# Context attention: the last tile of 49 keys folded to 256 columns on two partition halves

## The chip, the cores and the metric

The kernel runs on one core of a Trainium2 chip. Its engines are TensorE (PE; its weight loads are listed as PEld), VectorE (DVE), ScalarE (ACT), GpSimd (POOL) and SyncE (SP, which here only issues DMAs). Each engine runs its own list of instructions in order and waits on semaphores. The metric is the device time of one execution in microseconds.

## What is computed

The whole program is two transformer layers. Each has a cross-attention to a context of 1601 vectors per batch, a self-attention and a feed-forward part. The change touches only the cross-attention ("context attention"), which is done twice. Cut to what matters:

```
B, H, HD = 16, 16, 32                        # batches, heads, width of a head
y_main = y[:, :-16, :]                       # 1585 of 1601 context vectors, 256 wide
k = _ln((y_main @ Wk + bk) per head, kn_w, kn_b)     # 512 wide: 16 heads of 32
v = (y_main @ Wv + bv) per head
s = einsum('bhqd,bhkd->bhqk', q, k) * SCALE
p = softmax(s)
ctx = einsum('bhqk,bhkd->bhqd', p, v)        # plus the attention to the 16 others, done elsewhere
out = ctx @ Wo + bo
```

## The kernel before

`context_attention` treats one batch after another. The 1585 keys of a batch are cut into KT = 13 tiles: twelve of P = 128 keys and a last one, the tail, of TAIL = 49. Everything is kept as sums of two float16 parts, high and low, so that float16 matmuls give nearly float32 results.

For each tile i there is a chain of steps, and the names are those of the lists below. TensorE makes the K and V products (`k`, `v`, function `project`): for each of 2 slices of the 256 inputs and 3 combinations of parts it multiplies 128 keys by 512 columns of the weights, as two matmuls of 64 keys on the two column halves of the array, into `ps_k` and `ps_v`, of which there is one each. VectorE scales and adds the bias (`kc`, L452), ScalarE squares (`sq`, L367), VectorE sums by head (`rd`, L460), ScalarE makes a first guess of the inverse root (`r`, L373 and L377), GpSimd improves it by a Newton step (`nw`, L300 to L310), ScalarE puts it into the last columns of `ps_h` (`rp`, L384), VectorE multiplies (`hat`, L467), ScalarE writes the high part (`kh`, L392), VectorE the low part (`kl`, L475), and a transposing DMA issued by SP (L263) turns both into `kk`, with the 512 columns of K on partitions, four groups of 128. V needs ScalarE's high (`vh`, L400) and VectorE's low part (`vl`, L482).

The attention goes in 14 units of two tiles by half of the heads (`s`, L652, then the exponentials `e` on ScalarE, L420 and L422, the low part of the exponential `lo` on GpSimd, L335, and the product with V `pv`, L679). Units 6 and 13 hold only the tail: heads 0 to 7 in unit 6, heads 8 to 15 in unit 13. Ahead of that, first scores (`m`, L618) and their maxima on VectorE (L493, L496) give a shift per query.

For the tail, function `rows(i)` gives 49 instead of 128, so each of its matmuls and of its steps on VectorE and ScalarE works on 49 partitions and all 512 columns. The matmuls of the tail's products use only one column half of the array.

The order on each engine is the table ORDER, written out by hand. The number after a name is the tile or unit, and each "-" behind it moves it to an earlier batch. K and V of the next batch are made while the attention of the present one runs. The first line of TensorE's list reads as below. The change leaves the table as it is.

```
PE: pv2-- v9-- k12-- s4-- m3-- v10-- pv3-- s5-- m4-- k0- v11-- pv4-- m5-- s6-- k1- v12-- s7-- pv5-- m6--
```

## Time and profile before

| | |
|---|---|
| timed runs | 3058.69, 3063.67, 3066.0 us (median 3063.67) |
| profiled execution | 3058.08 us |
| its span in the trace | 3056.3 us |
| PE, DVE, ACT, POOL busy | 91%, 84%, 74%, 53% |
| the two context attentions | 101 to 1076 us and 1758 to 2731 us of the span |
| one batch inside them | 57.0 us |

How to read the views. The windows view has a line for each stretch: its length, then for each engine its busy time with the number of its instructions in brackets, the granted share of TensorE's clock, the share of the DMA engines and GB/s. The timeline has start and duration in us, engine, line, operation, what it writes and reads, shapes (partitions x elements; for a matmul also rows*columns of the loaded weights) and the number of instructions that the row merges; in brackets the idle time of the engine before it, where it is long enough to be listed, and what ended it. The groups of instructions have line, engine, operation, names, shapes, count, then busy us and mean ns of one, then idle time before them. Neighbouring rows of VectorE and ScalarE overlap by about 0.08 to 0.1 us when the engine doesn't wait.

### The profile page before, as it was taken

What the parts mean: (1) busy time and instruction counts of PE and PEld (TensorE: products, weight loads), DVE (VectorE), ACT (ScalarE), POOL (GpSimd) and SP (SyncE); (2) the same over time, 40 slices, a digit from 0 to 9 for tenths busy, and PEclk for the clock granted to TensorE, in tenths of its full rate; (3) what the DMA queues carried; (4) which work ended last, traced back from release to release, by engine and by line L of the source; (5) the groups of instructions that cost most, each with busy time, mean ns of one, the idle gap of its engine ahead of it and who ended that gap; (6) DMA issues with size and microseconds to landing.
All of it is one profiled execution on the core that took longest, in us unless ns stands there. A gap on an engine that the chain in (4) does not pass through costs nothing. (4 is left out here: it accounts for less than half of the span.)

```text
span 3056.3 us, 103347 instructions
## 1 busy us (share of the span) xinstructions
PE 2793.6 (91%) x42025; PEld 1761.7 (58%) x42025; DVE 2558.9 (84%) x4146; ACT 2268.2 (74%) x4155; POOL 1612.8 (53%) x2006
## 2 busy tenths in 40 slices
PE   7789999999999778789996779999999999968889
PEld 3346666666666556577774435666666666645646
DVE  6599999999999656768885779999999999957752
ACT  5479999999999754446664448999999999963431
POOL 1257777777777543212223326777777777752200
PEclk9899999999999889899998989999999999979989
DMA  4354654554554244348885345545545555430020
GB/s 127 86 96 84 98 91 87 97 88 88 96 89 83 56 160 153 133 165 302 302 305 152 102 88 87 98 87 89 96 89 90 94 89 96 75 91 1 1 75 28
DMA packets 542754, 329.52 MB, mean 108 GB/s; under 512 B 459382, under 2 KB 504566, under 8 KB 536523
## 3 DMA queue, kind: packets, MB, share of 16 engines
q1 hardware_dynamic: 534314, 295.63, 43.7%
q0 software_dynamic: 7680, 25.17, 2.7%
q8 instruction: 337, 5.52, 0.7%
q10 hardware_dynamic: 288, 2.10, 0.2%
q14 instruction: 135, 1.10, 0.1%
HBM read 181.86 MB, written 36.09 MB: 71 GB/s over the span
## 5 line engine op out<-in xcount | busy, mean ns | idle before, releaser
L335 POOL TENSOR_TENSOR a_elo<-a_e 128x1024 f16<-128x1024 f32 x428 | 854.5, 1997 | 272.4 <-ACT a_e L422 272.4
L592 PE MATMUL a_ps_k<-l_wk,a_yh 128*64 128x512 f16 (+1 forms) x3200 | 580.2, 386 | 32.2 <-POOL a_yl L317 22.0
L592 PE MATMUL a_ps_v<-l_wv,a_yh 128*64 128x512 f16 (+1 forms) x3200 | 577.5, 384 | 17.4 <-DVE a_v L482 16.8
L493 DVE TENSOR_REDUCE a_mx<-a_ps_m 128x2 f32<-128x1024 f32 x384 | 466.7, 1215 | 13.3 <-PE a_ps_m L618 12.0
L420 ACT ACTIVATE a_e<-a_ps_t 128x1024 f32<-128x1024 f32 x428 | 409.7, 957 | 33.6 <-PE a_ps_t L652 27.3
L422 ACT ACTIVATE a_e<-a_ps_t 128x1024 f16<-128x1024 f32 x428 | 410.8, 960 | 0.0
L652 PE MATMUL a_ps_t<-a_qb,a_kk 64*128 64x128 f16 (+1 forms) x9672 | 351.1, 219 | 8.1 <-ACT a_e L422 7.8
L652 PEld LDWEIGHTS a_ps_t<-a_qb,a_kk 64*128 64x128 f16 (+1 forms) x9672 | 281.5, 96 | 120.1 <-issue 88.6
L592 PE MATMUL a_ps_k<-l_wk,a_yl 128*64 128x512 f16 (+1 forms) x1600 | 322.6, 383 | 0.0
L592 PE MATMUL a_ps_v<-l_wv,a_yl 128*64 128x512 f16 (+1 forms) x1600 | 320.6, 380 | 0.0
L592 PEld LDWEIGHTS a_ps_k<-l_wk,a_yh 128*64 128x64 f16 (+1 forms) x3200 | 191.3, 110 | 221.1 <-issue 49.4
L452 DVE SCALAR_TENSOR_TENSOR a_kc<-a_ps_k,l_bk 128x512 f32<-128x512 f32 (+1 forms) x416 | 282.7, 680 | 41.6 <-PE a_ps_k L592 40.8
L592 PEld LDWEIGHTS a_ps_v<-l_wv,a_yh 128*64 128x64 f16 (+1 forms) x3200 | 191.1, 110 | 204.6 <-DVE a_v L482 33.4
L400 ACT ACTIVATE a_v<-a_ps_v 128x512 f16<-128x512 f32 (+1 forms) x416 | 255.8, 615 | 59.7 <-PE a_ps_v L592 45.5
L392 ACT ACTIVATE a_khl<-a_ps_h,a_one 128x512 f16<-128x512 f32 (+1 forms) x416 | 284.0, 683 | 17.7 <-DVE a_ps_h L467 15.0
L482 DVE SCALAR_TENSOR_TENSOR a_v<-a_ps_v,a_v 128x512 f16<-128x512 f32 (+1 forms) x416 | 284.3, 683 | 12.2 <-ACT a_v L400 10.4
L467 DVE TENSOR_TENSOR a_ps_h<-a_kc,a_ps_h 128x512 f32<-128x512 f32 (+1 forms) x416 | 285.8, 687 | 5.0 <-ACT a_ps_h L384 2.5
L679 PE MATMUL a_ps_o<-a_v,a_e 128*64 128x65 f16 (+1 forms) x6480 | 268.9, 199 | 20.6 <-POOL a_elo L335 16.9
L475 DVE SCALAR_TENSOR_TENSOR a_khl<-a_ps_h,a_khl 128x512 f16<-128x512 f32 (+1 forms) x416 | 282.9, 680 | 2.7 <-ACT a_khl L392 2.4
L679 PEld LDWEIGHTS a_ps_o<-a_v,a_e 128*64 128x64 f16 (+1 forms) x6480 | 239.9, 113 | 77.1 <-issue 37.5
L367 ACT ACTIVATE a_sq<-a_kc 128x512 f32<-128x512 f32 (+1 forms) x416 | 260.7, 627 | 24.7 <-DVE a_kc L452 24.0
L460 DVE TENSOR_REDUCE a_var<-a_sq 128x16 f32<-128x512 f32 (+1 forms) x416 | 277.7, 674 | 0.0
(415 smaller groups left out, 5316.0 us busy)
## 6 DMA issues: line engine op xcount, KB each, us to landing
l_land<-in_ctx SPq DMA_DIRECT2D x96, 384.0 KB, 3.8
l_ob<-in_m_w SPq DMA_DIRECT2D x32, 1024.0 KB, 7.9
f_w<-in_m_w SPq DMA_DIRECT2D x32, 512.0 KB, 4.9
eo_dram<-f_e_eo SPq DMA_DIRECT2D x32, 512.0 KB, 4.6
l_land<-in_ctx SPq DMA_DIRECT2D x32, 433.0 KB, 4.4
a_kk<-a_khl SPq DMA_TRANSPOSE x416, 3.1
qs_dram<-p_q SPq DMA_DIRECT2D x32, 128.0 KB, 2.4
dca_dram<-p_od SPq DMA_DIRECT2D x16, 256.0 KB, 2.4
```

Of the source, the lines that this page charges most:

```text
L335: pool.tensor_tensor(rest[0:r, :, 0:w], full[0:r, :, 0:w], high[0:r, :, 0:w], ALU.subtract)\
L392: act.activation(khl[0:r, n % 2, 0, :], ps_h[0:r, :], ACT.Identity, bias=one[0:r, 0:1])\
L420: act.activation(full[0:r, :, 0:w], src[0:r, :, 0:w], ACT.Exp)
L422: act.activation(high[0:r, :, 0:w], src[0:r, :, 0:w], ACT.Exp).then_inc(e_done, 1)
L452: dve.scalar_tensor_tensor(out=kc[0:r, kc_slot(at, i), :], in0=ps_k[0:r, :], scalar=1.0 / WSCALE, in1=bk[0:r, :], op0=ALU.mult, op1=ALU.ad ...
L467: dve.tensor_tensor(ps_h[0:r, :].rearrange("p (h d) -> p h d", d=HD), kc[0:r, kc_slot(at, i), :].rearrange("p (h d) -> p h d", d=HD), ps_h ...
L475: dve.scalar_tensor_tensor(out=khl[0:r, n % 2, 1, :], in0=ps_h[0:r, :], scalar=1.0, in1=khl[0:r, n % 2, 0, :], op0=ALU.add, op1=ALU.subtract)\
L482: dve.scalar_tensor_tensor(out=v[0:r, at.nbp, i, :, VLO:OW], in0=ps_v[0:r, :].rearrange("p (h d) -> p h d", d=HD), scalar=1.0 / WSCALE, in ...
L493: dve.tensor_reduce(mx[:, g, :, c], ps_m[:, :, :], AX.X, ALU.max).then_inc(mx_done, 1)
L592: m = pe.matmul(out[half:half + h, :], part[:, n % 2, c, o + half:o + half + h], w[:, wpart, c, :], start=(c == 0 and a == 0), stop=(c == ...
L652: t = pe.matmul(dst[0:rows(i), r, col:col + P], kk[d, at.bp, kpart + g, k], qb[d, at.bp, g, qpart, :, :].rearrange("p a q -> p (a q)"), st ...
L679: t = pe.matmul(ps_o[q, a * OW:a * OW + w], part[k, r, col + 64 * par:col + 64 * par + 64], v[k, at.bp, i, 2 * pair + par, 0:w], start=fir ...
```

## The change

Half of the tail's columns move to other partitions. Keys 0 to 48 with heads 0 to 7 (columns 0 to 255) stand on partitions 0 to 48, and the same keys with heads 8 to 15 (columns 256 to 511) on partitions 64 to 112. So `rows` gives 113 for the tail, and a new function `width` gives 256 columns for it instead of 512. `project` makes each step of the tail with two matmuls, 49 keys by 256 columns of the weights, one on each column half of the array. The steps `kc`, `sq`, `rd`, `hat`, `kh`, `kl`, `vh` and `vl` of the tail work on 256 columns. The bias in this form is a new tile `bt`, made by two copies on ScalarE at the start. The high and low parts of K stand side by side in 512 columns, so that one transposing DMA of 128 rows by 512 columns (before: 64 by 1024) brings them into a new tile `kt`. Scores, exponentials and values of unit 6 read and write partitions 0 to 48, those of unit 13 partitions 64 to 112, with the same numbers and sizes of matmuls. On GpSimd the low part of unit 13 runs over partitions 0 to 112. The instructions of each engine keep their order.

```diff
+        kk = sb("kk", [P, 2, 2 * GROUPS, (KT - 1) * P], F16)
+        kt = sb("kt", [P, 2, GROUPS, P], F16)
+        bt = sb("bt", [P, D // 2])
...
-            return P if i < KT - 1 else TAIL
+            return P if i < KT - 1 else 64 + TAIL
+
+        def width(i):
+            return D if i < KT - 1 else D // 2
+
+        def heads(i):
+            return width(i) // HD
+
+        def tail_rows(half):
+            return slice(64 * half, 64 * half + TAIL)
...
-            return (P, 512) if len(tiles_of(j)) == 2 else (TAIL, 256)
+            return (slice(0, P), 512) if len(tiles_of(j)) == 2 else (tail_rows(j // TPAIRS), 256)
...
                     if b >= 2:
                         sp.wait_ge(s_done, (b - 2) * UNITS + TPAIRS + i // 2 + 1)
-                    sp.dma_start_transpose(kk[:, b % 2, :, i * P:i * P + r],
-                                           khl[0:r, n % 2].rearrange("p a d -> p (a d)")).then_inc(turned[n % 2], 16)
+                    if i < KT - 1:
+                        sp.dma_start_transpose(kk[:, b % 2, :, i * P:(i + 1) * P],
+                                               khl[:, n % 2].rearrange("p a d -> p (a d)")).then_inc(turned[n % 2], 16)
+                    else:
+                        sp.dma_start_transpose(kt[:, b % 2], khl[:, n % 2, 0, :]).then_inc(turned[n % 2], 16)
...
+                for half in range(2):
+                    q = slice(64 * half, 64 * half + 64)
+                    act.activation(bt[q, :], bk[q, half * D // 2:(half + 1) * D // 2], ACT.Copy).then_inc(bt_ok, 1)
...
-                    dve.scalar_tensor_tensor(out=kc[0:r, kc_slot(at, i), :], in0=ps_k[0:r, :], scalar=1.0 / WSCALE,
-                                             in1=bk[0:r, :], op0=ALU.mult, op1=ALU.add).then_inc(kc_done, 1)
+                    bias, w = (bk, D) if i < KT - 1 else (bt, D // 2)
+                    if n == KT - 1:
+                        dve.wait_ge(bt_ok, 2)
+                    dve.scalar_tensor_tensor(out=kc[0:r, kc_slot(at, i), 0:w], in0=ps_k[0:r, 0:w], scalar=1.0 / WSCALE,
+                                             in1=bias[0:r, :], op0=ALU.mult, op1=ALU.add).then_inc(kc_done, 1)
...
                     dve.wait_ge(rp_done, n + 1)
-                    dve.tensor_tensor(ps_h[0:r, :].rearrange("p (h d) -> p h d", d=HD),
-                                      kc[0:r, kc_slot(at, i), :].rearrange("p (h d) -> p h d", d=HD),
-                                      ps_h[0:r, RSTD:D].unsqueeze(2).broadcast_to([r, H, HD]), ALU.mult)\
+                    w, hh = width(i), heads(i)
+                    dve.tensor_tensor(ps_h[0:r, 0:w].rearrange("p (h d) -> p h d", d=HD),
+                                      kc[0:r, kc_slot(at, i), 0:w].rearrange("p (h d) -> p h d", d=HD),
+                                      ps_h[0:r, w - hh:w].unsqueeze(2).broadcast_to([r, hh, HD]), ALU.mult)\
                        .then_inc(hat_done, 1)
...
-                            for half in range(0, r, 64):
-                                h = min(64, r - half)
-                                m = pe.matmul(out[half:half + h, :], part[:, n % 2, c, o + half:o + half + h], w[:, wpart, c, :],
-                                              start=(c == 0 and a == 0), stop=(c == KC - 1 and a == 2))
+                            for half in range(2):
+                                if i < KT - 1:
+                                    to, at_y, cols = slice(64 * half, 64 * half + 64), o + 64 * half, slice(0, D)
+                                else:
+                                    to, at_y, cols = tail_rows(half), o, slice(half * D // 2, (half + 1) * D // 2)
+                                m = pe.matmul(out[to, 0:width(i)], part[:, n % 2, c, at_y:at_y + to.stop - to.start],
+                                              w[:, wpart, c, cols], start=(c == 0 and a == 0), stop=(c == KC - 1 and a == 2))
...
                                 for r in range(2):
                                     d = slice(64 * r, 64 * r + 64)
-                                    t = pe.matmul(dst[0:rows(i), r, col:col + P], kk[d, at.bp, kpart + g, k],
+                                    keys = kk[d, at.bp, GROUPS * kpart + g, i * P:(i + 1) * P] if i < KT - 1 \
+                                        else kt[d, at.bp, 2 * kpart + gl, to]
+                                    t = pe.matmul(dst[to, r, col:col + P], keys,
                                                   qb[d, at.bp, g, qpart, :, :].rearrange("p a q -> p (a q)"),
```

## Rows read from the trace of the kernel before

**Rows 1.** The page, part 1: busy time of TensorE and of VectorE over the span.

```profile
PE 2793.6 (91%) x42025; PEld 1761.7 (58%) x42025; DVE 2558.9 (84%) x4146; ACT 2268.2 (74%) x4155; POOL 1612.8 (53%) x2006
```

**Rows 2.** Windows: PE, PEld, DVE, ACT, POOL busy; one batch, and the first attention's fill.

```profile
357.31:414.31 57.00, 56.92 (x1096) 34.89 (x1094) 56.30 (x91) 54.07 (x101) 43.10 (x55) 1.00 0.53 92
...
130.00:186.50 56.50, 42.57 (x346) 18.12 (x344) 54.61 (x81) 32.71 (x73) 16.98 (x41) 1.00 0.49 94
```

**Rows 3.** Timeline of PE and PEld: end of a V product, the tail's K product, next scores.

```profile
380.36 0.10 PEld L592 LDWEIGHTS a_ps_k<-l_wk,a_yh 128*49 128x49 f16 x1
...
380.36 0.39 PE L592 MATMUL a_ps_v<-l_wv,a_yh 128*64 128x512 f16 x2
380.57 0.38 PE L592 MATMUL a_ps_k<-l_wk,a_yh 128*49 128x512 f16 x1
...
381.65 0.38 PE L592 MATMUL a_ps_k<-l_wk,a_yh 128*49 128x512 f16 x1
381.96 0.23 PE L652 MATMUL a_ps_t<-a_qb,a_kk 64*128 64x128 f16 x2
```

**Rows 4.** Timeline of PE: 256 columns in the feed-forward part; a values unit, first and last.

```profile
1407.10 5.08 PE L2903 MATMUL f_e_ps_g<-f_e_gt,f_e_a 128*128 128x256 f16 x45
...
362.91 0.20 PE L679 MATMUL a_ps_o<-a_v,a_e 128*64 128x65 f16 x2
...
363.38 0.19 PE L679 MATMUL a_ps_o<-a_v,a_elo 128*64 128x33 f16 x2
```

**Rows 5.** Groups by shape on VectorE: longest and shortest tail form, a reduction of 256.

```profile
L467 DVE TENSOR_TENSOR a_ps_h<-a_kc,a_ps_h 49x512 f32<-49x512 f32 x32 | 21.7, 677 | 0.0
...
L460 DVE TENSOR_REDUCE a_var<-a_sq 49x16 f32<-49x512 f32 x32 | 21.4, 668 | 0.0
...
L1036 DVE TENSOR_REDUCE p_dmx<-p_ps_ds 128x16 f32<-128x256 f32 x16 | 6.7, 421 | 13.8 <-PE p_ps_ds L1363 13.8
```

**Rows 6.** Groups by shape on ScalarE: two tail forms, a copy of 256 columns.

```profile
L392 ACT ACTIVATE a_khl<-a_ps_h,a_one 49x512 f16<-49x512 f32 x32 | 21.6, 674 | 2.0 <-DVE a_ps_h L467 2.0
...
L400 ACT ACTIVATE a_v<-a_ps_v 49x512 f16<-49x512 f32 x32 | 19.3, 604 | 11.3 <-PE a_ps_v L592 11.2
...
L1222 ACT ACTIVATE p_pdt<-p_ps_pt 128x256 f32<-128x256 f32 x16 | 6.1, 380 | 4.3 <-PE p_ps_pt L1316 4.3
```

**Rows 7.** Timelines of ACT, PE and POOL, from the tail's V product to the values.

```profile
392.00 0.21 ACT L377 ACTIVATE a_r<-a_lnv 49x16 f32<-49x16 f32 x1
392.23 0.38 PE L592 MATMUL a_ps_v<-l_wv,a_yh 128*49 128x512 f16 x1
...
392.65 0.60 ACT L400 ACTIVATE a_v<-a_ps_v 49x512 f16<-49x512 f32 x1 [0.43 <-PE a_ps_v L592]
...
396.03 0.39 PE L618 MATMUL a_ps_m<-a_kk,a_qm 64*128 64x512 f16 x2
396.42 0.84 PE L652 MATMUL a_ps_t<-a_qb,a_kk 64*128 64x128 f16 x24
...
399.32 2.14 POOL L335 TENSOR_TENSOR a_elo<-a_e 128x1024 f16<-128x1024 f32 x1 [0.74 <-ACT a_e L422]
...
401.14 0.39 PE L618 MATMUL a_ps_m<-a_kk,a_qm 64*128 64x512 f16 x2
401.61 0.22 PE L679 MATMUL a_ps_o<-a_v,a_e 128*64 128x65 f16 x2
```

**Rows 8.** Timelines of ACT, DVE and PE, from an exponential to a V product.

```profile
371.53 1.03 ACT L420 ACTIVATE a_e<-a_ps_t 128x1024 f32<-128x1024 f32 x1
...
381.89 0.69 DVE L482 SCALAR_TENSOR_TENSOR a_v<-a_ps_v,a_v 128x512 f16<-128x512 f32 x1
...
382.95 0.41 PE L592 MATMUL a_ps_v<-l_wv,a_yh 128*64 128x512 f16 x2
```

**Rows 9.** The tile `kk`: time from issue to landing of its transposing DMAs.

```profile
DMA to landing us min/median/max: 2.6/3.1/5.7
```

More of the change, by code:

```diff
@@ L297, in newton_step @@
                     n, u, nt, r = at.nb * TPAIRS + p, (at.nbp * TPAIRS + p) % 2, len(tiles_of(p)), rows(2 * p)
[L298 removed]
+                    hh = heads(2 * p)
+                    v2, r2, a2, b2 = (t[0:r, u, 0:nt, 0:hh] for t in (var, r0, na, nb_))
                     pool.wait_ge(r0_done, n + 1)
[L300 removed]
+                    pool.tensor_tensor(a2, v2, eps[0:r, 0:nt * hh].rearrange("p (t h) -> p t h", h=hh), ALU.add)\
                         .then_inc(newton[0], 1)
@@ L334, in p_low @@
                     wait_values(pool, at, j)
-                    pool.tensor_tensor(rest[0:r, :, 0:w], full[0:r, :, 0:w], high[0:r, :, 0:w], ALU.subtract)\
+                    pool.tensor_tensor(rest[0:r.stop, :, 0:w], full[0:r.stop, :, 0:w], high[0:r.stop, :, 0:w],
+                                       ALU.subtract)\
                         .then_inc(lo_done, 1)
@@ L366, in square @@
                     need(act, red_done, n - 1)
-                    act.activation(sq[0:r, t, :], kc[0:r, kc_slot(at, i), :], ACT.Square, scale=SCALE).then_inc(sq_done, 1)
+                    w = width(i)
+                    act.activation(sq[0:r, t, 0:w], kc[0:r, kc_slot(at, i), 0:w], ACT.Square, scale=SCALE).then_inc(sq_done, 1)
                 def guess(at, p):
@@ L372, in guess @@
                     act.wait_ge(red_done, at.nb * KT + 2 * p + nt)
-                    act.activation(lnv[0:r, u, 0:nt, :], var[0:r, u, 0:nt, :], ACT.Ln, bias=eps[0:r, 0:1])\
+                    hh = heads(2 * p)
+                    act.activation(lnv[0:r, u, 0:nt, 0:hh], var[0:r, u, 0:nt, 0:hh], ACT.Ln, bias=eps[0:r, 0:1])\
                         .then_inc(ln_done, 1)
@@ L391, in k_high @@
                         act.wait_ge(turned[n % 2], 16 * (n // 2))
-                    act.activation(khl[0:r, n % 2, 0, :], ps_h[0:r, :], ACT.Identity, bias=one[0:r, 0:1])\
+                    w = width(i)
+                    act.activation(khl[0:r, n % 2, 0, 0:w], ps_h[0:r, 0:w], ACT.Identity, bias=one[0:r, 0:1])\
                         .then_inc(kh_done, 1)
@@ L459, in variance @@
                     need(dve, newton[4], at.nb * TPAIRS + p - 1)
-                    dve.tensor_reduce(var[0:r, (at.nbp * TPAIRS + p) % 2, i % 2, :], sq[0:r, t, :].rearrange("p (h d) -> p h d", d=HD), AX.X, ALU.add)\
+                    dve.tensor_reduce(var[0:r, (at.nbp * TPAIRS + p) % 2, i % 2, 0:heads(i)],
+                                      sq[0:r, t, 0:width(i)].rearrange("p (h d) -> p h d", d=HD), AX.X, ALU.add)\
                        .then_inc(red_done, 1)
@@ L474, in k_low @@
                     dve.wait_ge(kh_done, n + 1)
-                    dve.scalar_tensor_tensor(out=khl[0:r, n % 2, 1, :], in0=ps_h[0:r, :], scalar=1.0,
-                                             in1=khl[0:r, n % 2, 0, :], op0=ALU.add, op1=ALU.subtract)\
+                    w = width(i)
+                    part = khl[0:r, n % 2].rearrange("p a d -> p (a d)")[:, w:2 * w]
+                    dve.scalar_tensor_tensor(out=part, in0=ps_h[0:r, 0:w], scalar=1.0,
+                                             in1=khl[0:r, n % 2, 0, 0:w], op0=ALU.add, op1=ALU.subtract)\
                        .then_inc(kl_done, 1)
@@ L540, in low @@
                     wait_values(dve, at, j)
-                    dve.tensor_tensor(rest[0:r, :, 0:w], full[0:r, :, 0:w], high[0:r, :, 0:w], ALU.subtract)\
+                    dve.tensor_tensor(rest[r, :, 0:w], full[r, :, 0:w], high[r, :, 0:w], ALU.subtract)\
                        .then_inc(low_done, 1)
@@ L644, in scores @@
                     for i in tiles_of(j):
-                        k = slice(i * P, i * P + rows(i))
+                        to = slice(0, P) if i < KT - 1 else tail_rows(half)
                         for gl in range(2):
@@ L667, in values @@
                     for i in tiles_of(j):
-                        k = slice(0, rows(i))
+                        k = slice(0, P) if i < KT - 1 else tail_rows(half)
+                        h0 = 0 if i < KT - 1 else H // 2 * half
                         for gl in range(2):
```

36 lines of the change are left out of this document (18 added, 18 removed).

## The prediction

> **What bounds the kernel now.** I read the page's busy shares first, then the windows view over one batch, then the timeline of single engines inside that batch, and last the groups of instructions by shape. The page gives TensorE 91% and VectorE 84% of the span [rows 1]; these are means over very different stages, so they say only where to look. The windows view says more. In the two context attentions one batch follows another every 57.00 us, and in such a stretch TensorE is busy for 56.92, VectorE for 56.30, ScalarE for 54.07 and GpSimd for 43.10 us, at a granted clock of 1.00 [rows 2]. Two engines are full, and a third nearly so. A busy TensorE proves little by itself, since the ends of matmuls are modelled; the spacing of their starts is the proof. A pair of 64-row matmuls of 512 columns holds the engine for 0.21 us (380.36 to 380.57), and so does each of the six single matmuls of the tail's product, which start from 380.57 to 381.65; the next group, which uses another split of the array, starts 0.31 us after the last [rows 3]. I followed such starts through the batch, and nearly all are that dense. The exceptions are two: the scores of 396.42 come 0.39 us after a pair of 512 columns that needs 0.22, and the values of 401.61 come 0.47 us after one that needs 0.31 (rows 3's step with a change of split) [rows 7]. That is 0.17 + 0.15 = 0.32 us of waiting. TensorE's own work is thus 57.00 - 0.32 = 56.68 us a batch.
>
> **What the change takes away on TensorE.** Before, the tail's K and V products are six matmuls each of 49 rows by 512 columns: 6 x 0.216 = 1.30 us each, half the array's columns idle. Now they are six pairs of 49 rows by 256 columns, on the two halves of the array. What does a pair of 256 columns cost? No row shows exactly that. The nearest rows: a matmul of 256 columns of the same type on the whole array, 45 in 5.08 us, so (5.08 - 0.27) / 44 = 109 ns from start to start; and the pairs of the values, 64 rows each with 65 and 33 columns, 16 pairs from 362.91 to 363.38, so 31 ns a pair with two weight loads and different moving data on the two halves [rows 4]. Two halves with different data do run beside each other, loads and all, and 31 ns is far below 109. From above, the two matmuls of a pair one after the other would be 218 ns, which is what is there now; from below, 107 ns, half of 0.214. I take 109, nearest to both rows. A product then takes 6 x 0.109 = 0.65 us, and a batch saves 2 x 0.65 = 1.29 us. Scores, first scores and values of the tail keep their numbers and sizes of matmuls, only partitions and array halves differ: nothing.
>
> Weighed against a page: the rows of the values show 15 ns per matmul with a weight load each [rows 4]. The Trainium skill, "TensorE: Matmul & The Clock Gate", section "Back-to-back issue gap", says that in a real stream of load and matmul the spacing is about 81 ns per matmul at 128 columns and 131 at 512. A straight line between them gives an estimate of 98 ns at 256, hence 12 x 98 = 1.18 us for a product and only 0.24 us saved a batch on TensorE. It speaks against this change; I give it little weight because 15 ns is far under its floor.
>
> **On VectorE.** Five instructions a batch shrink from 512 to 256 columns (centred K, variance, normalised K, low part of K, low part of V). The tail forms last 668 to 677 ns; a reduction of 256 columns lasts 421 ns [rows 5]. 5 x (0.672 - 0.424), with 0.003 added for operands in PSUM, is 1.24 us. VectorE is bound in the fill, where it is busy for 54.61 of 56.50 us [rows 2]; the saving counts there in place of TensorE's.
>
> **On ScalarE.** Square, high part of K and high part of V shrink. The forms last 674 (K) and 604 ns (V); a copy of 256 columns out of PSUM lasts 380 [rows 6]. That is 0.22 us for V; for the other two, by the same slope, 0.21 each: 0.65 us a batch. The exponentials keep 512 columns.
>
> **Small things.** The 8 instead of 16 heads in the guess, the root and GpSimd's Newton steps save tens of nanoseconds beside other work: 0. GpSimd's low part for the second tail unit reads 113 partitions instead of 49 at the same width; its time goes by width, and it is idle for 14 us of the batch [rows 2]: 0. The bias is copied twice at the start of each attention (two ScalarE copies of 256 columns, 0.8 us at [rows 6]), while the first context chunk is still on its way, and VectorE waits for it only at its first tail, long after: 0; if that cover were gone it would be 2 x 0.8 = 1.6 us in all. The tail's transposing DMA moves 128 rows of 512 columns instead of 64 rows of 1024, the same bytes and half of a usual one; landings of all sizes take 2.6 to 5.7 us, 3.1 in the middle [rows 9]. I take 0; the bound is 0.4 us either way, the space between 2.6 and the usual 3.1, and it isn't waited for at once. No instruction changes its place in any engine's order.
>
> **Which loops are left.** All engines run fixed lists, so the period is that of the slowest loop through the semaphores. Four are close.
> (a) TensorE alone: 56.68 - 1.29 = 55.39 us.
> (b) The loop with the waits seen today: V tail product (last start 392.23) -> V's high part on ScalarE at 392.65, which waited 0.43 us for it -> ScalarE's list up to the scores' exponentials -> scores 396.42 -> exponentials -> GpSimd 399.32 for 2.14 us, ending 401.46 -> values 401.61 -> TensorE to the next batch [rows 7]. Its length is the full 57.00. It loses both products' 1.29 and V's 0.22: 55.49.
> (c) The same without TensorE's tail: ScalarE's own list is busy until 392.21, 0.02 us before that last product starts, and V's high part can move up by the 0.53 us from there to 392.65 plus the usual overlap of 0.1 [rows 7]. So 57.00 - 0.53 - 0.22 (V) - 0.21 (square) = 56.04, less what ScalarE idles elsewhere on the way, which its timeline lets me estimate at up to 0.24: 55.80 to 56.04.
> (d) ScalarE runs without a break from its exponential at 371.53 to the root that VectorE's normalised K waits for, VectorE's low part of V follows at 381.89 and ends at 382.58, and the next V product starts at 382.95, where TensorE would take it from about 382.64 on [rows 8]. That loop has 0.31 us to spare, misses the K tail product and loses only the V one: 57.00 - 0.31 - 0.65 = 56.04; on its way it also skips the 0.32 us of waits or takes V's 0.22: 55.72 to 55.82.
> VectorE alone is below: 56.30 - 1.24 = 55.06, or 55.76 if all its idle 0.70 us stays [rows 2].
> So the period falls to between 55.4 and 56.04, and the late ones decide: I take 55.85, a gain of 1.15 us. Late next is ScalarE, not TensorE.
>
> **The sum.** Each attention does 16 tails, two attentions 32: 32 x 1.15 = 36.8 us. The profiled execution took 3058.1 us (span 3056.3), hence 3021.3. The timed runs lie at 3058.7, 3063.7 and 3066.0, the median 5.6 above the profiled one. I add half of that difference: 3024 us.
>
> **The rivals.**
> 1. A wait that I didn't find takes the saving's place. ScalarE and VectorE are idle for 2.9 and 0.7 us of a batch, in small pieces [rows 2], and fixed lists may interlock otherwise with other durations. Half of the gain remains: 32 x 0.5 = 16 us, 3045 on the same footing. For it: (c) and (d) are already such loops. Against: in every loop that I followed some tail instruction stands. Chance 0.11, spread over gains from 8 to 22 us.
> 2. The pair of 256 columns takes 218 ns, one after the other; the change doesn't do on TensorE what it says. (a) stays at 56.68, the gain is 0.32 x 32 = 10 us: 3051. By the page above, with its 0.24 us, it would be 0.56 x 32 = 18 us and 3043. Against both: rows 4. Chance 0.05.
> 3. Slower: the weight loads come into the open. A load of 49 columns lasts 0.10 us [rows 3] and is hidden today under 0.216 us of streaming; now two of them have to hide under 0.109. If each matmul waited for its own, a pair would take 2 x (0.109 + 0.10) = 0.42 us, 12 pairs 2.4 us more a batch, so 56.68 + 2.4 = 59.1, and 32 x 2.1 = 67 us: 3128. It turns into a loss once a pair takes over 0.216 + 0.32 / 12 = 0.243 us. Against: the values' pairs, 31 ns with their loads. Chance 0.03.
> 4. Nothing moves, because what holds the period is a loop with no tail instruction at all: within 6 us of 3061. Against: all four loops above have one. Chance 0.03.
>
> **How the numbers follow.** The forecast (gains of 22 to 51 us, periods of 55.4 to 56.3) has 0.78. Gains of under 0.2% (6 us, about what a measurement of this kernel can tell from no change) come from rival 4 and the end of rivals 1 and 2. Faster 0.93, same 0.04, slower 0.03. The range reaches from 3058.7 - 51 = 3008 to 3066 - 22 = 3044, and takes in part of rival 1.
>
> **What would show it.** In the profile after: starts of the tail's products 0.11 us apart by pairs; VectorE's tail forms near 425 ns and ScalarE's near 385 to 460; windows of about 55.85 us, with TensorE waiting some 0.4 us more per batch than today, in front of the V product of (d) or the scores and values of (b); V's high part of the tail no longer idle for 0.43 us. Wrong would be: pairs at 0.2 us (rivals 2, 3), or windows over 56.3 us with pairs at 0.11 (rival 1).

## The result, and the profile after

The changed kernel takes 3028.76 us (median of 4 runs, 3025.69 to 3031.59) against 3062.49 us for the kernel before: a ratio of 0.989, with a 95% interval of 0.9873 to 0.9907. Its profiled execution took 3027.51 us, with a span of 3025.7. A second comparison (run `after_again`, 5 runs against 23 of the kernel before), gave 3030.5 against 3056.84 us, a ratio of 0.9923 (0.991 to 0.9936): 26 us saved and not 34. The first ratio flatters the change somewhat. The prediction said 3024, between 3008 and 3044. The time and the direction hold, and the small saving that it announced on each engine is there; the step from these savings to the period of a batch does not hold, and most of what follows is about that step.

First the sizes. The page's busy line, which answers [rows 1]:

```profile
PE 2762.7 (91%) x42409; PEld 1765.6 (58%) x42409; DVE 2521.2 (83%) x4146; ACT 2247.9 (74%) x4159; POOL 1613.7 (53%) x2006
```

The windows view over one batch of each context attention, which answers [rows 2] (PE, PEld, DVE, ACT, POOL busy, each with its count, the granted clock, the DMA share, GB/s):

```profile
351.31:407.36 56.05, 55.74 (x1108) 34.85 (x1104) 55.08 (x90) 53.30 (x101) 42.98 (x55) 1.00 0.56 93
687.95:744.01 56.06, 55.68 (x1108) 34.81 (x1106) 55.14 (x91) 53.41 (x101) 43.06 (x55) 1.00 0.52 93
```

VectorE's 1.24 us a batch is gone from 56.30 (55.08 and 55.14 now), ScalarE's 0.65 from 54.07 (53.30 and 53.41). The timeline of TensorE at the tail's K product, which answers [rows 3]:

```profile
711.21 0.28 PE L626 MATMUL a_ps_k<-l_wk,a_yh 128*49 128x256 f16 x2
711.32 0.28 PE L626 MATMUL a_ps_k<-l_wk,a_yl 128*49 128x256 f16 x2
711.43 0.39 PE L626 MATMUL a_ps_k<-l_wk,a_yh 128*49 128x256 f16 x4
...
711.97 0.84 PE L689 MATMUL a_ps_t<-a_qb,a_kk 64*128 64x128 f16 x24
```

The two matmuls of a pair start together, and pair follows pair by 0.11 us (711.21, 711.32, 711.43). The scores start 0.76 us after the first pair, where the tail of before needed 381.96 - 380.57 = 1.39. The difference is 0.63 to 0.65 us for a product, as predicted. The groups by shape on VectorE, ScalarE and GpSimd (busy us, mean ns of one, idle before), which answer [rows 5] and [rows 6]:

```profile
L495 DVE TENSOR_TENSOR a_ps_h<-a_kc,a_ps_h 113x256 f32<-113x256 f32 x32 | 13.3, 416 | 0.4 <-ACT a_ps_h L406 0.4
...
L486 DVE TENSOR_REDUCE a_var<-a_sq 113x8 f32<-113x256 f32 x32 | 13.0, 406 | 0.0
...
L415 ACT ACTIVATE a_khl<-a_ps_h,a_one 113x256 f16<-113x256 f32 x32 | 15.3, 477 | 1.0 <-DVE a_ps_h L495 1.0
...
L387 ACT ACTIVATE a_sq<-a_kc 113x256 f32<-113x256 f32 x32 | 14.6, 457 | 0.0
...
L423 ACT ACTIVATE a_v<-a_ps_v 113x256 f16<-113x256 f32 x32 | 12.5, 391 | 2.4
...
L350 POOL TENSOR_TENSOR a_elo<-a_e 113x512 f16<-113x512 f32 x30 | 34.8, 1161 | 0.9 <-ACT a_e L445 0.9
L350 POOL TENSOR_TENSOR a_elo<-a_e 49x512 f16<-49x512 f32 x30 | 34.5, 1150 | 17.1 <-ACT a_e L445 17.1
```

The lines shown for VectorE are its longest and its shortest tail form; all five lie between 406 and 416 ns (424 was taken). 113 partitions instead of 49 cost GpSimd 11 ns. The idle time of 11.3 us ahead of the tail's high part of V [rows 6] is down to 2.4, as loop (b) said it would be.

Now the period. It is read from the start of the reduction of the maxima (L534), which comes once a batch, here on VectorE's timeline:

```profile
687.95 0.17 DVE L534 TENSOR_REDUCE a_mxx<-a_mx 128x8 f32<-128x32 f32 x1
...
744.01 0.17 DVE L534 TENSOR_REDUCE a_mxx<-a_mx 128x8 f32<-128x32 f32 x1
```

So this batch takes 56.06 us. Over 26 batches (13 of each attention) the most frequent value is 56.04 to 56.07, the mean 56.15; before, 57.00 and 57.03. A batch of the most frequent length is called calm below. The gain is 0.95 us in a calm batch and 0.88 in the mean, where 1.15 was predicted. Of the span's 30.6 us, 2 x 15 periods make 26.6. The other 4 us lie outside these periods, and the profiles show how little they mean. From the last values of the first attention to the first K product of the second, a stretch in which only the two bias copies are new, TensorE's timeline has 689.4 us before and 689.1 in the changed kernel, but 691.5 in a second profile of the same changed kernel (span 3027.0), and 684.5 to 693.3 over all 14 profiles. The first attention's fill, from its first K product to its first L534, has 78.8 us before and 78.3 and 77.0 in the two profiles of the changed kernel. So single times can differ by several us for reasons that no change here touches, and the experiments are read by their periods.

Two waits stand on TensorE's timeline where there was slack (time to spare) before:

```profile
712.65 0.38 PE L653 MATMUL a_ps_m<-a_kk,a_qm 64*128 64x512 f16 x2
713.25 0.41 PE L626 MATMUL a_ps_v<-l_wv,a_yh 128*64 128x512 f16 x2 [0.22 <-DVE a_v L513]
...
714.36 0.38 PE L626 MATMUL a_ps_v<-l_wv,a_yh 128*64 128x512 f16 x2
714.75 0.22 PE L717 MATMUL a_ps_o<-a_v,a_e 128*64 128x65 f16 x2
```

The V product of tile 10 starts 0.60 us after the first scores instead of 0.31, that is loop (d) of the prediction, announced. The values of unit 3 start 0.39 us after the last group of that product; before they started 0.21 after it. That wait, 0.18 us, was in no step of the prediction. It leads back through GpSimd and ScalarE, whose timelines are:

```profile
709.48 0.26 POOL L315 TENSOR_TENSOR a_na<-a_var,a_eps 128x32 f32<-128x32 f32 x1 [0.24 <-ACT a_r L398]
...
710.71 0.25 POOL L325 TENSOR_TENSOR a_rstd<-a_r,a_na 128x32 f32<-128x32 f32 x1
710.92 1.59 POOL L332 TENSOR_TENSOR a_yl<-l_land,a_yh 128x768 f16<-128x768 f32 x1
712.47 2.14 POOL L350 TENSOR_TENSOR a_elo<-a_e 128x1024 f16<-128x1024 f32 x1
```

```profile
702.16 1.02 ACT L443 ACTIVATE a_e<-a_ps_t 128x1024 f32<-128x1024 f32 x1
...
709.17 0.23 ACT L398 ACTIVATE a_r<-a_lnv 128x32 f32<-128x32 f32 x1
709.30 0.67 ACT L415 ACTIVATE a_khl<-a_ps_h,a_one 128x512 f16<-128x512 f32 x1
```

ScalarE's root guess ends at 709.40, GpSimd refines it, then makes the low part of the context (ends 712.51), then the low part of the exponentials of unit 3 (712.47 + 2.14 = 714.61), and the values start 0.14 us later. GpSimd is idle for 13 us of the batch, and still it is on the path here: between those two points its list holds nothing but the refining steps, each waiting for the one before it, and the two low parts. Before, the same steps left a little to spare, as the timelines of GpSimd and TensorE of before show:

```profile
381.84 2.14 POOL L335 TENSOR_TENSOR a_elo<-a_e 128x1024 f16<-128x1024 f32 x1
```

```profile
384.06 0.38 PE L592 MATMUL a_ps_v<-l_wv,a_yh 128*64 128x512 f16 x2
384.27 0.20 PE L679 MATMUL a_ps_o<-a_v,a_e 128*64 128x65 f16 x2
```

**The loop through GpSimd** closes like this (a loop is a chain of steps and hand-overs from one batch to the same step of the next; the period can't be shorter than the longest): scores of unit 8 -> their exponentials on ScalarE (727.00 to 728.94) -> their low part on GpSimd (729.02 to 731.16) -> values of unit 8 (731.30) -> TensorE to the scores of unit 1 of the next batch -> ScalarE without a break from the exponentials of unit 1 to the root -> GpSimd as above -> values of unit 3 -> TensorE with the tail's V product to the scores of unit 8. Its length can be had from the trace of before: 57.00 us less the 0.15 us that the values of unit 3 had to spare (384.27 against 381.84 + 2.14 + 0.14) and the 0.17 us that the scores waited at 396.42 [rows 7] makes 56.68. It bypasses the K product and VectorE altogether, so all it loses is one product: 56.68 - 0.65 = 56.03 us, and 56.04 is the period measured.

It isn't alone. **A loop through the exponentials of unit 4** has the same stretch of ScalarE and no step of GpSimd for unit 3: ScalarE goes on from the root to the exponentials of unit 4, and their end lets TensorE start the scores of unit 5; from there on it is the loop above. ScalarE's and TensorE's timelines of before:

```profile
382.16 0.71 ACT L392 ACTIVATE a_khl<-a_ps_h,a_one 128x512 f16<-128x512 f32 x1
382.85 1.03 ACT L420 ACTIVATE a_e<-a_ps_t 128x1024 f32<-128x1024 f32 x1
383.77 1.01 ACT L422 ACTIVATE a_e<-a_ps_t 128x1024 f16<-128x1024 f32 x1
```

```profile
384.87 0.84 PE L652 MATMUL a_ps_t<-a_qb,a_kk 64*128 64x128 f16 x24
```

and of the changed kernel:

```profile
714.26 1.06 ACT L445 ACTIVATE a_e<-a_ps_t 128x1024 f16<-128x1024 f32 x1
```

```profile
715.37 0.40 PE L689 MATMUL a_ps_t<-a_qb,a_kk 64*128 64x128 f16 x8
```

In the changed kernel these scores start 0.05 to 0.06 us after the exponentials end (714.26 + 1.06), with nothing to spare. Before, they had 0.03 (384.87 against 383.77 + 1.01 + 0.06), and the exponentials had waited some 0.12 themselves: they start 0.69 us after the high part of K, where 0.57 is usual (713.35 - 712.78 in the changed kernel). So this loop was 57.00 - 0.03 - 0.12 - 0.17 = 56.68 long, and with one product less it is again 56.03. Both loops could be read from the trace of before, and in the changed kernel both bind at once.

### The profile page after: what moved, and what is told of

Same layout as the page of the kernel before. It is cut to its first block and busy times, and to the rows that moved or that the text cites. A ratio compares the mean times of both kernels' runs of the same rounds, so it can differ in the third digit from the quotient of the medians.

```text
span 3025.7 us, 104119 instructions
## 1 busy us (share of the span) xinstructions
PE 2762.7 (91%) x42409; PEld 1765.6 (58%) x42409; DVE 2521.2 (83%) x4146; ACT 2247.9 (74%) x4159; POOL 1613.7 (53%) x2006
## 5 line engine op out<-in xcount | busy, mean ns | idle before, releaser
L626 PE MATMUL a_ps_k<-l_wk,a_yh 128*64 128x512 f16 (+1 forms) x3328 | 564.1, 378 | 32.2 <-POOL a_yl L332 21.9
L626 PE MATMUL a_ps_v<-l_wv,a_yh 128*64 128x512 f16 (+1 forms) x3328 | 561.4, 376 | 22.1 <-DVE a_v L513 20.9
L689 PE MATMUL a_ps_t<-a_qb,a_kk 64*128 64x128 f16 x8928 | 319.3, 219 | 8.1 <-ACT a_e L445 8.0
L689 PEld LDWEIGHTS a_ps_t<-a_qb,a_kk 64*128 64x128 f16 x8928 | 260.9, 95 | 84.1 <-issue 53.8
L478 DVE SCALAR_TENSOR_TENSOR a_kc<-a_ps_k,l_bk 128x512 f32<-128x512 f32 x384 | 261.0, 680 | 43.8 <-PE a_ps_k L626 43.0
L415 ACT ACTIVATE a_khl<-a_ps_h,a_one 128x512 f16<-128x512 f32 (+1 forms) x416 | 276.8, 665 | 16.0 <-DVE a_ps_h L495 14.3
L513 DVE SCALAR_TENSOR_TENSOR a_v<-a_ps_v,a_v 128x512 f16<-128x512 f32 (+1 forms) x416 | 275.5, 662 | 14.1 <-ACT a_v L423 11.8
L495 DVE TENSOR_TENSOR a_ps_h<-a_kc,a_ps_h 128x512 f32<-128x512 f32 (+1 forms) x416 | 276.9, 666 | 9.0 <-ACT a_ps_h L406 6.9
L505 DVE SCALAR_TENSOR_TENSOR a_khl<-a_ps_h,a_khl 128x512 f16<-128x512 f32 (+1 forms) x416 | 275.2, 662 | 4.2 <-ACT a_khl L415 2.1
L486 DVE TENSOR_REDUCE a_var<-a_sq 128x16 f32<-128x512 f32 (+1 forms) x416 | 269.6, 654 | 0.0
```

Source lines behind the costliest of these rows:

```text
L415: act.activation(khl[0:r, n % 2, 0, 0:w], ps_h[0:r, 0:w], ACT.Identity, bias=one[0:r, 0:1])\
L486: dve.tensor_reduce(var[0:r, (at.nbp * TPAIRS + p) % 2, i % 2, 0:heads(i)], sq[0:r, t, 0:width(i)].rearrange("p (h d) -> p h d", d=HD), AX ...
L495: dve.tensor_tensor(ps_h[0:r, 0:w].rearrange("p (h d) -> p h d", d=HD), kc[0:r, kc_slot(at, i), 0:w].rearrange("p (h d) -> p h d", d=HD), ...
L505: dve.scalar_tensor_tensor(out=part, in0=ps_h[0:r, 0:w], scalar=1.0, in1=khl[0:r, n % 2, 0, 0:w], op0=ALU.add, op1=ALU.subtract)\
L513: dve.scalar_tensor_tensor(out=v[0:r, at.nbp, i, 0:hh, VLO:OW], in0=ps_v[0:r, 0:w].rearrange("p (h d) -> p h d", d=HD), scalar=1.0 / WSCAL ...
L626: m = pe.matmul(out[to, 0:width(i)], part[:, n % 2, c, at_y:at_y + to.stop - to.start], w[:, wpart, c, cols], start=(c == 0 and a == 0), s ...
```

## The experiments

Each ratio is to the kernel before on the same chip; its median was 3055.9 to 3056.8 us there, lower than the 3062.49 of the first comparison. `rd_full`, `k3_full`, `wide_v`, `wide_k` and `swap_pool` ran once each, so their times say little. Periods are from starts of L534, have 26 batches each behind them and hold for calm ones. The expectations call a wait of TensorE a stay.

**The parts one by one.** `pe_wide` undoes TensorE's part: the first half's matmuls have 512 columns again (the second half's still run beside them), and the unused columns are computed for nothing.

```
-    m = pe.matmul(out[to, 0:width(i)], part[:, n % 2, c, at_y:at_y + to.stop - to.start],
+    wide = half == 0
+    wc = D if wide else width(i)
+    if wide:
+        cols = slice(0, D)
+    m = pe.matmul(out[to, 0:wc], part[:, n % 2, c, at_y:at_y + to.stop - to.start],
```

> Of the changed kernel, TensorE's part undone alone: in the tail's K and V products the matmul on the lower half of the array runs over all 512 columns of the weights again (the upper 256 columns of its result are never used), so a pair holds TensorE for 0.216 us instead of 0.109; VectorE and ScalarE keep their 256 columns. The changed kernel has a period of 56.05 us per batch and 3028.8 us in all. Theory E (a loop through VectorE's tail variance and the low part of K, tile 11, sets the period; it misses both tail products on TensorE): the period rises only until TensorE's own work, 55.39 + 1.29 = 56.68 us, is the longest: 56.7 us, +20 us, about 3049. Rival D (the loop over VectorE's low part of V, tile 9, and the V product of tile 10): it has the tail's V product in it, 56.04 + 0.65 = 56.7, the same. Rival V (TensorE doesn't matter any more): 56.05 and 3029.

Measured: 3049.34 us, ratio 0.9973 (0.9961 to 0.9985). The period, again from VectorE's timeline (582.24 to 639.06), is 56.82 us, 0.12 over what two of the theories expected: VectorE's and ScalarE's 1.9 us together are worth 0.18 us a batch. What is left is TensorE with its one wait, for GpSimd's low part ahead of the values of unit 8: 57.00 - 0.17 = 56.83.

`va_full` keeps TensorE's part and undoes the others: the tail's five steps on VectorE and three on ScalarE run over 512 columns of 113 partitions, half of them without meaning (the same edit in most steps; the bias and the high part of K are read twice over).

```
-    w = width(i)
+    w = D
...
-    w, hh = width(i), heads(i)
+    w, hh = D, H
```

> The other way round: TensorE's part of the change alone. The tail's products are folded as in the changed kernel, but all of VectorE's and ScalarE's tail steps (centred K, variance, normalised K, high and low parts of K and V, square) run over 512 columns again, the upper 256 unused. Theory E: +0.26 us for the tail's variance and +0.19 for the centred K, which stand in the loop: 56.3 to 56.5 us per batch, +8 to +14 us on 3028.8. Rival D: none of the two stands in it, but V's high part (+0.21) may, by the loop over ScalarE: 56.05 to 56.25, 0 to +6 us. Rival A (TensorE alone counts): 56.05, 3029.

Measured: 3051.56 us, ratio 0.9989 (0.9979 to 0.9998), period 56.69. The expectation missed, its highest theory (E) by 0.2 to 0.4 us; the timelines of TensorE and VectorE show why:

```profile
673.57 0.39 PE L664 MATMUL a_ps_m<-a_kk,a_qm 64*128 64x512 f16 x2
674.17 0.41 PE L637 MATMUL a_ps_k<-l_wk,a_yh 128*64 128x512 f16 x2 [0.21 <-DVE a_kc L479]
```

```profile
672.84 0.69 DVE L501 TENSOR_TENSOR a_ps_h<-a_kc,a_ps_h 128x512 f32<-128x512 f32 x1
673.43 0.68 DVE L479 SCALAR_TENSOR_TENSOR a_kc<-a_ps_k,l_bk 128x512 f32<-128x512 f32 x1
```

Here a K product waits for the centred K of the tile before (ends 674.11), 0.3 us beyond the usual 0.31 after the scores, and that wait is not there in the changed kernel. VectorE at its old length seems to have a loop of its own at 56.69; no run shows that loop by itself. By its period this kernel should be some 4 us faster than `pe_wide`, and it took 2 us more: that is within what the work outside the batches varies by. So TensorE alone gains 0.31 us a batch, the other two alone 0.18, and both together 0.95: in nearly every loop of before, the other engine's saving was needed too.

**Which TensorE work counts.** `wide_v` and `wide_k` widen one of the two products only.

```
+    wide = half == 0 and done is v_done        # wide_v
+    wide = half == 0 and done is k_done        # wide_k
```

> The changed kernel with only the tail's V product on TensorE wide again (a pair holds it for 0.216 us, 0.65 us more a batch). After the first runs there are two candidates for the 56.04 us: theory F, a loop that goes through GpSimd's low part of exponential unit 3, the values of unit 3 on TensorE, the tail's V product, the scores of unit 8 and back through ScalarE and GpSimd; and theory E, the loop through VectorE's tail variance (by the runs with VectorE's steps undone, 55.99 us long). F has the tail's V product in it: 56.04 + 0.65 = 56.7 us. E doesn't: TensorE's own list with its stay at GpSimd, 55.55 + 0.65 = 56.2 us, would be the longest.

> The same with only the tail's K product wide, which stands ahead of the values of unit 3, where loop F enters TensorE. Theory F: the period rises only to TensorE's own 56.2 us, +0.15. A theory in which TensorE's work as such sets the period: 56.05 + 0.65 = 56.7 us, the same as with the V product.

Both add 32 x 0.65 us of TensorE time; the groups by shape of `wide_v` and of `wide_k` show one kind of product at 512 columns each:

```profile
L630 PE MATMUL a_ps_v<-l_wv,a_yh 128*49 128x512 f16 x128 | 43.3, 379 | 1.2 <-DVE a_v L513 1.2
```

```profile
L630 PE MATMUL a_ps_k<-l_wk,a_yh 128*49 128x512 f16 x128 | 43.3, 379 | 0.3 <-DVE a_kc L478 0.3
```

Measured: 3041.39 us and a period of 56.69 with the wide V product, 3035.16 us and 56.19 with the wide K product. The V product comes back in full (+0.65), the K product with 0.15. That is what the loop through GpSimd asks for, which holds the V product and bypasses the K product: 56.04 + 0.65 = 56.69, and 56.19 is TensorE with its one wait, 56.83 - 0.65 = 56.18. A TensorE that is slow as such would have given the same for both, and the loop through VectorE 56.2 for the V product. The loop through the exponentials of unit 4 also holds the V product and bypasses the K product, so these two runs can't tell it from the one through GpSimd.

**A step of VectorE.** `rd_full` sums the tail's variance over 512 columns, `k3_full` does its centred, normalised and low K so.

```
-    sq[0:r, t, 0:width(i)].rearrange("p (h d) -> p h d", d=HD), AX.X, ALU.add)
+    sq[0:r, t, :].rearrange("p (h d) -> p h d", d=HD), AX.X, ALU.add)
```

> The changed kernel with one instruction a batch undone: the tail's variance on VectorE reduces 512 columns again (16 heads, the upper 8 unused), 0.26 us more. It runs between the low part of K of tile 8 and that of tile 11. Theory E: the period rises by all of it, 56.05 to 56.31 us. Rival D: nothing, 56.05, since the low part of V of tile 9 comes ahead of it and the rest of that loop runs on TensorE. Rival A: 56.05.

> The changed kernel with three of VectorE's tail steps undone: centred K, normalised K and the low part of K run over 512 columns again, 0.8 us more in all. Normalised K and the low part of the tail come after the low part of K, tile 11, where theory E's loop leaves VectorE; the centred K comes just before the low part of tile 8, where that loop enters, with 0.08 us to spare. Theory E: 56.05 + 0.26 - 0.08 = 56.23 us. Rival D: 56.05. Rival V (VectorE's whole load sets the period): 56.05 + 0.8 = 56.85.

Measured: 3036.42 us with a period of 56.25, and 3041.78 us with 56.18. One step of VectorE longer by 0.26 us makes the period longer by 0.21: that fits a loop through VectorE of 56.25 - 0.26 = 55.99, just under the 56.04. Its far end is on ScalarE's timeline of the changed kernel, at the tail's roots:

```profile
726.34 0.18 ACT L406 ACTIVATE a_ps_h<-a_rstd 113x8 f32<-113x8 f32 x1 [0.30 <-DVE a_khl L505]
...
727.00 1.03 ACT L443 ACTIVATE a_e<-a_ps_t 128x1024 f32<-128x1024 f32 x1
```

The low part of K of tile 11 holds up the roots, and they, but for a few hundredths, the exponentials of unit 8. `k3_full` has three long steps and yet only 56.18. One of the three on that loop's stretch and the others beside it (55.99 + 0.2) would fit; no run splits them. Its time is 6.6 us above that of `wide_k` with the same period; 4.8 us of that lie behind the second attention (from its last values to the end 330.4 us against 325.6), where the two kernels are the same.

**Taking the GpSimd wait away.** `swap_pool` turns the two GpSimd steps round, so that the values of unit 3 get their low part 1.6 us earlier. `swap_both` besides puts the low K of tile 11 ahead of a maximum on VectorE, and the scores of unit 8 ahead of those of the maxima on TensorE.

```
-    POOL: ... nw4- yl0 lo3- lo4- ...
+    POOL: ... nw4- lo3- yl0 lo4- ...
     swap_both also:
-    DVE: ... rd0- m6-- kl11-- ...      PE: ... pv6-- m7-- s8-- v0- ...
+    DVE: ... rd0- kl11-- m6-- ...      PE: ... pv6-- s8-- m7-- v0- ...
```

> The changed kernel with two steps of GpSimd's list exchanged: the low part of exponential unit 3 ahead of the low part of the context's chunk 0. Theory F: unit 3 ends 0.57 us earlier, the values of unit 3 no longer wait 0.18 us, and the loop is 55.9 us; but E's loop of 55.99 us stays: the period falls from 56.05 to 55.99 us. Without F: no change, or a longer period where the context part comes late (56.05 or more).

> Both loops cut: GpSimd's exchange of the run before, and the low part of K, tile 11, ahead of the maximum 6 on VectorE, with the scores of unit 8 ahead of first scores 7 on TensorE. If E and F are the two longest, the period falls below 55.99 us, to where the wait of the V product of tile 10 for VectorE's low part of V stands, about 55.85 us: 0.2 us a batch, 6 us in all on 3028.8, ratio to the kernel before 0.987. If other loops of 56.0 us exist, it stays at 55.95 to 56.05.

Measured: 3031.38 us with 56.06, and 3030.26 us (ratio 0.9919, 0.9905 to 0.9932) with 56.09: no gain, where 55.99 and 55.85 had been expected. The timelines of TensorE and ScalarE of `swap_pool`:

```profile
715.19 0.38 PE L626 MATMUL a_ps_v<-l_wv,a_yh 128*64 128x512 f16 x2
...
716.21 0.29 PE L689 MATMUL a_ps_t<-a_qb,a_kk 64*128 64x128 f16 x4
```

```profile
715.09 1.06 ACT L445 ACTIVATE a_e<-a_ps_t 128x1024 f16<-128x1024 f32 x1
```

The values' wait is gone as meant (they start 0.21 us after the product again), but TensorE then stands before the scores of unit 5 until 716.21, because the exponentials of unit 4 end at 716.15. That is the loop through the exponentials of unit 4. It alone keeps the period at 56.06, so the loop through GpSimd is not the only cause of 56.04. The changed kernel sits in a nest of loops between 55.99 and 56.06.

**Moving work out of ScalarE's stretch.** All of these pass ScalarE from the exponentials of unit 1 to those of unit 3 or 4. `tuned` takes two steps out of it, the high part of the context (`yh0`) and the square of tile 11, and turns GpSimd round too; `tuned2` adds the two swaps of `swap_both`. The changed kernel ran again beside them.

```
-    ACT: ... rp7- yh0 r4- kh7- e3- rp8- vh9- sq11- kh8- e4- rp9- ...
+    ACT: ... rp7- r4- kh7- e3- rp8- vh9- kh8- yh0 e4- sq11- rp9- ...
```

> The changed kernel itself, again, so that the reordered one stands beside it on the same chip. Every theory expects 3028.8 us (3025.7 to 3031.6 so far) and a period of 56.04 us in most batches, with 0.1 us more in the mean.

> The changed kernel with two orders rewritten: on ScalarE the high part of the context goes behind the exponentials of unit 3 and the square of tile 11 behind those of unit 4 (both were ahead of the exponentials of unit 3, that is, in the unbroken stretch of ScalarE from unit 1 to unit 4), and on GpSimd the low part of the exponentials of unit 3 goes ahead of the low part of the context. Theory of loops: every loop of 56.0 to 56.05 us found so far (through GpSimd to the values of unit 3, through VectorE's low V to the V product, through VectorE to the roots at the end of the batch, through the exponentials of unit 4 to the scores of unit 5) runs through that stretch of ScalarE; the two steps are 0.77 and 0.52 us in it, so these loops fall by 0.5 to 0.8 us, and what is left is ScalarE with its stays, worked out as 55.86 us, and TensorE alone with 55.55 us: a period of 55.85 to 55.95 us, a time of about 3024 us, 4 to 6 us under the changed kernel in the same job. Rival: what sets 56.04 us is no loop of that kind but friction that comes with any tight order (TensorE's own stays): the period stays within 0.03 us of 56.04 us, and the time within 1 us of the changed kernel. A period above 56.1 us would say that the high part of the context, which now comes later, is itself waited for (by the transposes of the context on TensorE).

> The kernel of the run before, and besides the low K of tile 11 ahead of the sixth of the maxima on VectorE and the scores of unit 8 ahead of the seventh values step on TensorE, as in the run that swapped both. Theory of loops: these two only shorten loops that the rewritten ScalarE order has shortened already, so no gain beside the run before, within 0.03 us of its period. If the loop through VectorE to the roots is still the longest there, this one is shorter by up to 0.1 us per batch, 3 us in all.

Measured: 3030.5 us for the changed kernel, 3059.13 for `tuned` (ratio 1.0007, 0.9999 to 1.0016) and 3056.47 for `tuned2` (0.9999, 0.9988 to 1.0011), periods 56.07, 56.95 and 56.88. Neither theory is right: the reordered kernel gives the whole gain back. ScalarE's and VectorE's timelines of `tuned`:

```profile
604.64 0.69 ACT L415 ACTIVATE a_khl<-a_ps_h,a_one 128x512 f16<-128x512 f32 x1 [0.22 <-DVE a_ps_h L495]
...
608.16 0.69 ACT L415 ACTIVATE a_khl<-a_ps_h,a_one 128x512 f16<-128x512 f32 x1 [0.37 <-DVE a_ps_h L495]
608.74 0.83 ACT L380 ACTIVATE a_yh<-l_land 128x768 f16<-128x768 f32 x1
609.48 1.01 ACT L443 ACTIVATE a_e<-a_ps_t 128x1024 f32<-128x1024 f32 x1
```

```profile
611.95 0.69 DVE L486 TENSOR_REDUCE a_var<-a_sq 128x16 f32<-128x512 f32 x1 [1.18 <-ACT a_sq L387]
```

The two steps that I took out stood exactly where ScalarE hands a root to VectorE and needs the normalised K back. In the changed kernel they fill that round trip; without them ScalarE idles 0.22 and 0.37 us ahead of the two high parts of K. By the starts on the changed kernel's ScalarE timeline the two steps hold the list for 0.73 and 0.52 us. Of these 1.25 us some 0.6 come straight back so, and 0.74 come in again with `yh0` ahead of the exponentials of unit 4 (608.74 to 609.48). The square, now behind these, makes VectorE wait for 1.18 us. This is read from the timelines: no run moves one of the two steps alone, so how the 0.9 us are shared between them isn't shown. A list without gaps is not a list whose every step lengthens the loop.

**Making the stretch really shorter.** `sq_short` leaves all orders alone and squares only 64 of the 512 columns of tiles 9 and 10 (the expectation says 1024, a slip), both in that stretch; the rest of these squares is left out.

```
-    w = width(i)
+    w = 64 if i in (9, 10) else width(i)
```

> The changed kernel in its own orders, with the squares of tiles 9 and 10 on ScalarE over 64 columns instead of 1024 (the other columns of their variances are summed from what the buffer held: work is left out). The two squares are the third and the sixth step of ScalarE's stretch from the exponentials of unit 1 to those of unit 4, and no step of another engine is moved. Theory of loops: all loops of 55.9 to 56.05 us found so far run through that stretch; it gets 0.8 us shorter, so they fall to about 55.2, and what is left is TensorE with its own stays (55.55 us) and VectorE (about 55.3 us, 56.05 less the waits that its rows show): a period of 55.5 to 55.75 us, a time of 3012 to 3020 us. Theory of waits, from the reordered kernel before: the squares stand where ScalarE would otherwise wait for VectorE (the centred K with its roots multiplied in, 0.35 us a time), so what is taken off the squares comes back as waits of ScalarE: a period of 56.0 us or more and a time within 3 us of 3030 us. Rival of friction (TensorE's own stays set 56.04 us): also 56.04 us, but with ScalarE's exponentials of unit 4 ending earlier and no wait on their way.

Measured: 3021.95 us (3018.28 to 3027.74), ratio 0.9895 (0.9879 to 0.9912), and a period of 55.83 in calm batches. Fewer batches are calm here, and the mean is 56.07 against 56.15: over all periods some 4 us. The ratio to before, 0.9895, is lower than the 0.9923 of `after_again` by more than that, and again the rest lies outside: the work between the attentions took 684.5 us in this profile. ScalarE's timeline:

```profile
702.91 1.02 ACT L443 ACTIVATE a_e<-a_ps_t 128x1024 f32<-128x1024 f32 x1
...
704.74 0.26 ACT L387 ACTIVATE a_sq<-a_kc 128x64 f32<-128x64 f32 x1
704.88 0.69 ACT L415 ACTIVATE a_khl<-a_ps_h,a_one 128x512 f16<-128x512 f32 x1
705.82 1.02 ACT L443 ACTIVATE a_e<-a_ps_t 128x1024 f32<-128x1024 f32 x1 [0.25 <-PE a_ps_t L689]
...
708.13 0.26 ACT L387 ACTIVATE a_sq<-a_kc 128x64 f32<-128x64 f32 x1
708.43 0.19 ACT L406 ACTIVATE a_ps_h<-a_rstd 128x16 f32<-128x16 f32 x1
...
709.69 0.23 ACT L398 ACTIVATE a_r<-a_lnv 128x32 f32<-128x32 f32 x1
```

The squares fall from 0.65 to 0.26 us, 0.78 together. But from the exponentials of unit 1 to the root guess ScalarE now takes 709.69 - 702.91 = 6.78 us, against 709.17 - 702.16 = 7.01 in the changed kernel: 0.23 us less. The rest has turned into waits, 0.25 us for the scores of unit 2 above all, and some ahead of the roots at 708.43. What arrives at the end of the stretch is what the period loses (56.04 to 55.83). So this stretch of ScalarE does bound a calm batch, and friction of TensorE, which would have kept 56.04, is refuted; but the next bound, TensorE's scores of unit 2 among it, lies at 55.83, not at 55.5 to 55.75 as I expected.

## Why the prediction was right, and where not

- **TensorE's saving: right.** Pairs 0.11 us apart, a product 1.30 to 0.65 us. The loads of 0.10 us [rows 3] stay hidden, and rivals 2 and 3 are refuted. The prediction's estimate of 1.18 us a product, from the Trainium skill, "TensorE: Matmul & The Clock Gate", section "Back-to-back issue gap", is not what the trace shows: 0.65 us.
- **VectorE's and ScalarE's own savings: right.** 406 to 416 ns against 424, and 457, 477 and 391 ns against 460, 460 and 380.
- **Small things: right.** The two bias copies take 0.85 us at 99.94 us, while ScalarE would wait for the context chunk; GpSimd's wider partitions cost 11 ns.
- **The list of loops: this step failed.** The prediction took 55.85 from loops (c) and (d). Missing were the loop through GpSimd's low part for unit 3 and the one through the exponentials of unit 4. Both were to be seen in the trace of before: they had 0.15 us each to spare, less than the 0.95 by which everything else moved. I had asked only who waits today, not who is about to. Their lengths by the rows of before come to 56.03, the timelines of the changed kernel show both without slack, and `wide_v` and `wide_k` bear out what both contain. `swap_pool` shows that the second sets 56.06 by itself; whether the first would do so alone, no run shows. Just behind them stands the loop through VectorE (55.99, from `rd_full`). All three were over the 55.83 of `sq_short`, so all three must pass the stretch of ScalarE that this run shortened.
- **Loop (a): a slip of the same step.** The 0.32 us of waits were taken off TensorE's own work (by the rows shown 0.47 - 0.31 is 0.16, so 0.33; it changes nothing). But 0.15 of them, ahead of the values of unit 8, are part of a loop that goes from TensorE's scores through ScalarE and GpSimd back to it; only 0.17 were slack. That loop is 56.83 us before (seen in `pe_wide`, 56.82) and 56.83 - 1.29 = 55.54 after. It bounded nothing in the end.
- **Loop (d): nearly right.** The V product does wait, 0.29 us, as announced. Of the 0.32 us of waits only the 0.17 ahead of the scores of unit 8 can be skipped, so the loop is 57.00 - 0.31 - 0.17 - 0.65 = 55.87 us and not 55.72 to 55.82. In the changed kernel the 0.18 us that the values of unit 3 wait for GpSimd are its slack: 56.04 - 0.18 = 55.86. By this loop alone the predicted 55.85 would have held. That the measured 56.04 is also the upper bound of (c) and (d) is a coincidence of numbers for (d); for (c) no run settles it.
- **The sum.** 36.8 us were predicted for the batches, the 30 periods between starts of L534 gave 26.6. Of the difference of 10.2, to within 0.2, 30 x 0.20 = 6.0 us is the calm period (1.15 against 0.95), 30 x 0.07 = 2.1 us the irregular batches (0.88 in the mean against 0.95), and 2 x 1.15 = 2.3 us the two batches that lie in fill and drain. What makes batches irregular is not settled. The long ones are up to 0.7 us over the calm ones, and they are not all chance: the thirteenth period of the first attention (856.32 to 912.64 in the changed kernel, 56.32 us) is 0.2 us or more over the calm ones in 12 of the 14 profiles. Against that, 4 us came from outside the periods, mostly chance, and half of the 5.6 us between profile and median was added where 1.25 was right. So it is in part luck that the forecast missed the time by only 5 us, while the batches fell short by 10; in the other comparison the kernel saves 26 us, where the forecast had 36.8 for the batches.
- **Rival 1** (a hidden wait takes part of the saving) was thus the mechanism, at a sixth of the gain in a calm batch instead of a half. The range was wide enough because it priced that rival.

## What to carry to other kernels

When several engines run fixed lists in a loop, write the period as the longest loop through the semaphores, and list not only the waits seen but every hand-over with less slack than the gain hoped for, those of idle engines too. A saving on one full engine may be worth little until the others are cut as well (0.31 and 0.18 us alone, 0.95 together). And before a step is moved out of an unbroken stretch, ask which round trip it fills there.

## What the runs showed of the hardware

- Two 49-row matmuls of 256 columns with different moving data, on the two halves of the array, start together, pair after pair 0.11 us apart (711.21, 711.32), each with its own weight load of 49 columns.
- On VectorE, 256 columns cost 406 to 416 ns over 113 partitions, and 512 columns 668 to 677 ns over 49 [rows 5]: the width counts, 1.0 ns a column and some 0.15 us besides, and the partitions hardly do (512 columns over 128 partitions: 674 to 688 ns). Steps without a wait follow each other 0.07 to 0.09 us before the one ahead has ended in the record, so that a step costs the list a little less than its duration.
- A square of 64 columns takes ScalarE 0.26 us, of 512 columns 0.65 (`sq_short` and the changed kernel).
